# A two-layer graph block on one core: the barrier of 8 turned tiles a batch added by VectorE instead of TensorE

## The reference, cut to what matters

```python
h = relu(layernorm(x))
x = x + L0(h, adj)        # attention over the graph's edges, 8 heads of 16
h = relu(layernorm(x))
x = x + L1(h, adj)        # two similarity graphs on the same edges

# L0
q, k, v = split(h @ W_qkv + b_qkv)
scores = where(adj, q @ k.T / sqrt(16), -inf)     # per head, 512 x 512
y = softmax(scores) @ v ;  out = y @ W_out + b_out

# L1
z_l, z_g, v = h @ Wl, h @ Wg, h @ Wv
A_l = max(cos(z_l, z_l), 0)  without diagonal, only on edges
A_g = exp(-|z_g - z_g'|^2 / 2)  without diagonal, only on edges
K = 0.9 * A_l / rowsum(A_l) + 0.1 * A_g / rowsum(A_g)
out = K @ v @ Wo
```

## Time and profile before

| | |
|---|---|
| median of 3 runs | 866.05 us |
| the profiled execution | 870.53 us |
| its span, first to last instruction | 868.8 us |
| mean granted TensorE clock | 0.986 |
| TensorE matmuls busy | 799.0 us (92%), 4732 |
| weight loads busy | 450.8 us (52%) |
| VectorE busy | 684.9 us (79%), 1950 |
| ScalarE busy | 544.1 us (63%), 1230 |
| GpSimd busy | 707.4 us (81%), 829 |
| moved by DMA | 54.7 MB, 63 GB/s in the mean |

### The profile page before, as it was taken

One profiled execution on the slowest core, in us unless ns is written; L12 is line 12 of the kernel. 1 busy time (PEld: TensorE's weight loads), 2 busy tenths in 40 slices (PEclk: granted clock), 3 DMA queues, 4 the chain that ended last, 5 costly groups with the idle time before them and its releaser, 6 DMA issues.

```text
span 868.8 us, 15316 instructions
## 1 busy us (share of the span) xinstructions
PE 799.0 (92%) x4732; PEld 450.8 (52%) x4732; DVE 684.9 (79%) x1950; ACT 544.1 (63%) x1230; POOL 707.4 (81%) x829
## 2 busy tenths in 40 slices
PE   3769799999999999999999999999999999999886
PEld 2222245646464555656465564646455565645466
DVE  4666669888897979788796978879797988779266
ACT  4536495765758486674848566575857667575832
POOL 3268999797989889898888979898898989877921
PEclk9888999999999999999999999999999999999999
DMA  3331313113131412312141221303131231210000
GB/s 89 105 103 38 104 38 95 48 50 101 27 94 38 116 38 72 82 48 80 27 116 38 81 74 50 99 21 102 38 115 39 61 93 41 67 36 14 13 1 25
DMA packets 49840, 54.74 MB, mean 63 GB/s; under 512 B 7264, under 2 KB 43616, under 8 KB 49760
## 3 DMA queue, kind: packets, MB, share of 16 engines
q1 hardware_dynamic: 49760, 53.76, 22.0%
HBM read 30.28 MB, written 23.07 MB: 61 GB/s over the span
## 4 chain that ended last, share of the span: by engine, by line
PE 35%; POOL 30%; DMA 12%; DVE 8%; issue 7%; ACT 5%; SPq 2%; POOLq 0%; DVEq 0%; ACTq 0%
POOL probs_t L547 17%; PE adj L722 6%; DMA qk_rows<-k_dram 6%; PE pv L708 6%; PE score L680 5%; PE turned L694 4%; DMA k_dram<-split 4%; PE adj L717 4%; POOL split L579 3%; PE work L740 3%; POOL x_resid L615 2%; DVE scrap L955 2%; POOL split L577 2%; PE work L717 2%; PE turned L693 1%
## 5 line engine op out<-in xcount | busy, mean ns | idle before, releaser
L547 POOL TENSOR_TENSOR probs_t<-probs_t,keep_t 128x512 int32<-128x512 int32 x384 | 493.2, 1314 | 15.6 <-ACT probs_t L1126 15.5
L1126 ACT ACTIVATE probs_t<-turned 128x512 f32<-128x512 f32 x512 | 298.5, 603 | 186.1 <-PE turned L694 183.1
L955 DVE CUSTOM_DVE_ANT_0 scrap<-score,mask_add 128x512 f32<-128x512 f32 x512 | 341.0, 682 | 61.0 <-PE score L680 58.3
L680 PE MATMUL score<-qk_rows 96*128 96x512 bf16 x512 | 199.3, 389 | 15.1 <-DMA qk_rows<-k_dram 13.0
L694 PE MATMUL turned<-qk_rows 99*128 99x512 bf16 x512 | 196.5, 384 | 14.6 <-ACT probs_t L1126 12.4
L708 PE MATMUL pv<-probs_t,v_cols 128*32 128x512 f32 x1024 | 139.0, 615 | 3.9 <-POOL probs_t L547 3.9
L680 PEld LDWEIGHTS score<-qk_rows 96*128 96x128 bf16 x512 | 49.8, 97 | 131.0 <-DVE neg_max L955 58.0
L694 PEld LDWEIGHTS turned<-qk_rows 99*128 99x128 bf16 x512 | 50.7, 99 | 47.3 <-ACT probs_t L1126 22.7
L988 DVE SCALAR_TENSOR_TENSOR adj_rbf<-rbf_exp,mask_t 128x512 f32<-128x512 f32 x64 | 74.4, 1164 | 1.0 <-ACT rbf_exp L1160 1.0
L722 PEld LDWEIGHTS adj<-v_cos,adj_cos 128*128 128x128 f32 x480 | 61.4, 190 | 12.1 <-issue 4.7
L722 PE MATMUL adj<-v_cos,adj_cos 128*128 128x129 f32 x480 | 64.6, 276 | 0.7 <-DVE out_sb L1011 0.7
(11 more groups left out here) (159 smaller groups left out, 1188.4 us busy)
## 6 DMA issues: line engine op xcount, KB each, us to landing
q_dram<-split SPq DMA_DIRECT2D x96, 128.0 KB
qk_rows<-q_dram SPq DMA_DIRECT2D x32, 384.0 KB, 3.9
k_dram<-split SPq DMA_DIRECT2D x48, 128.0 KB
qk_rows<-k_dram SPq DMA_DIRECT2D x32, 192.0 KB, 4.3
x_sb<-in_x_dram SPq DMA_DIRECT2D x16, 256.0 KB, 3.5
qk_rows<-k_dram SPq DMA_DIRECT2D x32, 128.0 KB, 4.2
out_dram<-out_sb SPq DMA_DIRECT2D x15, 256.0 KB, 2.5
qk_rows<-k_dram SPq DMA_DIRECT2D x32, 64.0 KB, 4.4
```

The costliest lines, as they stand in the source:

```text
L547: pool.tensor_tensor(tile, tile, keep_t[:, w // HG % T, :], ALU.mult).then_inc(probs_masked.sem, 1)
L680: pe.matmul(score_bank[u % 2][:, :], qk_rows[0:ROWS, b % 2, 0, h, t * P:(t + 1) * P], qk_rows[0:ROWS, b % 2, 1, h, :], start=True, stop=Tr ...
L955: dve.tensor_tensor_reduce(scrap[:, u % 2, :], score_bank[u % 2][:, :], mask_add[:, u % T, :], -1.0, 3.0e38, ALU.add, ALU.min, neg_max[:, ...
L1126: act.activation(probs_t[:, k % 4, w % HG, :], turned_bank[w % 2][:, :], ACT.Exp, scale=SCALE).then_inc(probs_ready.sem, 1)
```

## The change

For the tiles with `w % 4 == 3` the matmul of the barrier is gone (`MASK_BY_PE` is empty; `MASK_BY_DVE` has them). VectorE reads the turned tile from its bank, adds `bar_t` and writes the sum to a new SBUF tile `barred`, of which there is one; the exp reads that. TensorE's turned tile two later waits for this add instead of the exp. The add stands in VectorE's list in the tile's own slot, right behind the scan of the slot. The scan's unused output `scrap` becomes bf16. And many entries of `AT` move, most by one slot, some by more: `k_split` from -9 to -14, `x_biased` from -14 to -12, on SyncE `qk_store` from -28 to -35, `rows` from (-8, -5) to (-27, -12), `x_next` from -24 to -31, `max_load` from (1, 25) to (-4, 17), `store` from 99 to 106. `AT_BEFORE_LAST` and `AT_LAST` stay.

```diff
-MASK_BY_PE = (3,)
+MASK_BY_PE = ()
+MASK_BY_DVE = (3,)
@@ AT
-    "hT": (-26,), "q": (-24,), "k": (-22,), "v": (-12,), "max_turn": (18, 32),
+    "hT": (-26,), "q": (-24,), "k": (-22,), "v": (-13,), "max_turn": (18, 32),
-    "z": (69, 71, 72, 73), "zgT": (76,), "col": (78,), "zlT": (79,), "rbf": (78, 83, 85, 87),
-    "cos": (81, 83, 84, 89), "mix_cos": (92, 95, 96, 97), "mix_rbf": (94, 95, 96, 98),
-
-    "ln_scale": (-28,), "hT_copy": (-26,), "q_hi": (-24,), "k_hi": (-22,), "max_copy": (18, 32),
-    "pv_copy": (42, 56), "yT_copy": (61,), "ln2_scale": (64,), "h2T_hi": (66,), "z_copy": (70, 71, 72, 74),
-    "z_sums": (71, 72, 74, 75), "zgT_hi": (75,), "col_copy": (78,), "zlT_hi": (79,), "rbf_exp": (80, 83, 87, 89),
-
-    "ln_moments": (-35,), "hT_split": (-26,), "q_rest": (-24,), "k_rest": (-21,), "v_add": (-12,),
-    "max_split": (13, 30), "y_scale": (57, 59), "x1": (62,), "ln2_moments": (63,), "h2T_lo": (67,),
-    "zgT_lo": (76,), "zlT_lo": (79,), "rbf_read": (78, 83, 85, 88), "cos_read": (81, 83, 87, 90),
-    "rbf_mask": (83, 84, 88, 92), "out": (94, 96, 97, 101),
-
-    "ln_rstd": (-31,), "q_split": (-23,), "k_split": (-9,), "x_biased": (-14,), "ln2_rstd": (62,),
-    "z_norms": (76,),
-
-    "qk_store": (-28,), "rows": (-8, -5), "x_next": (-24,), "max_load": (1, 25), "store": (99,),
+    "z": (70, 71, 72, 73), "zgT": (76,), "col": (78,), "zlT": (79,), "rbf": (79, 82, 84, 87),
+    "cos": (82, 83, 85, 90), "mix_cos": (93, 96, 97, 98), "mix_rbf": (94, 96, 97, 99),
+
+    "ln_scale": (-29,), "hT_copy": (-27,), "q_hi": (-25,), "k_hi": (-22,), "max_copy": (18, 31),
+    "pv_copy": (42, 57), "yT_copy": (59,), "ln2_scale": (65,), "h2T_hi": (66,), "z_copy": (70, 71, 72, 74),
+    "z_sums": (70, 72, 74, 75), "zgT_hi": (75,), "col_copy": (78,), "zlT_hi": (79,), "rbf_exp": (80, 82, 87, 89),
+
+    "ln_moments": (-37,), "hT_split": (-26,), "q_rest": (-24,), "k_rest": (-21,), "v_add": (-12,),
+    "max_split": (14, 30), "y_scale": (57, 59), "x1": (62,), "ln2_moments": (63,), "h2T_lo": (67,),
+    "zgT_lo": (77,), "zlT_lo": (80,), "rbf_read": (78, 83, 85, 88), "cos_read": (81, 83, 87, 90),
+    "rbf_mask": (83, 84, 88, 92), "out": (94, 97, 98, 100),
+
+    "ln_rstd": (-31,), "q_split": (-24,), "k_split": (-14,), "x_biased": (-12,), "ln2_rstd": (62,),
+    "z_norms": (77,),
+
+    "qk_store": (-35,), "rows": (-27, -12), "x_next": (-31,), "max_load": (-4, 17), "store": (106,),
@@ tiles
+        scrap = sb("scrap", [P, 2, N], BF16)
+        barred = sb("barred", [P, N])
@@ turned_scores (TensorE)
-                reached(pe, probs_ready, b, w - 1)
+                if (w - 2) % SLOTS in by_dve:
+                    reached(pe, barred_ready, *((b, by_dve.index(w - 2) + 1) if w >= 2 else (b - 1, len(by_dve))))
+                else:
+                    reached(pe, probs_ready, b, w - 1)
@@ VectorE, behind the scan of the slot
+                if hit := tile_due(s, LAG):
+                    b, w = hit
+                    if w in by_dve:
+                        reached(dve, turned_filled, b, w + 1)
+                        if w >= HG:
+                            reached(dve, probs_ready, b, w - HG + 1)
+                        else:
+                            reached(dve, probs_ready, b - 1, w - HG + 1 + SLOTS)
+                        dve.tensor_tensor(barred[:, :], turned_bank[w % 2][:, :], bar_t[:, w // HG % T, :],
+                                          ALU.add).then_inc(barred_ready.sem, 1)
@@ exp (ScalarE)
+                    src = turned_bank[w % 2]
+                    if w in by_dve:
+                        reached(act, barred_ready, b, by_dve.index(w) + 1)
+                        src = barred
+                    act.activation(probs_t[:, k % 4, w % HG, :], src[:, :], ACT.Exp,
```

More of the change, by code:

```diff
@@ L107, in graph_blocks @@
     by_pe = [w for w in range(SLOTS) if w % HG in MASK_BY_PE]
-    by_pool = [w for w in range(SLOTS) if w % HG not in MASK_BY_PE]
+    by_dve = [w for w in range(SLOTS) if w % HG in MASK_BY_DVE]
+    by_pool = [w for w in range(SLOTS) if w not in by_pe and w not in by_dve]
     def slots_of(name, batch):
@@ L182, in graph_blocks @@
         v_cols = sb("v_cols", [P, 3, T, H, 32])
-        scrap = sb("scrap", [P, 2, N])
+        scrap = sb("scrap", [P, 2, N], BF16)
+        barred = sb("barred", [P, N])
         neg_max = sb("neg_max", [P, GROUPS, HALF])
@@ L295, in graph_blocks @@
         turned_filled = signal("turned_filled", SLOTS)
+        barred_ready = signal("barred_ready", len(by_dve))
         probs_ready = signal("probs_ready", SLOTS)
@@ L701, in attend @@
                 reached(pe, probs_masked, b, sum(w < ends for w in by_pool))
-                if by_pe:
-                    reached(pe, probs_ready, b, 1 + max(w for w in by_pe if w < ends))
+                reached(pe, probs_ready, b, 1 + max(w for w in by_pe + by_dve if w < ends))
                 if j == 0:
@@ L874, in _ @@
                         reached(pe, probs_ready, b)
+                        reached(pe, barred_ready, b)
                     split_product(z_bank(b, t)[:, 0:3 * D],
@@ L1125, in _ @@
                         reached(act, pv_filled, b, k - 3)
-                    act.activation(probs_t[:, k % 4, w % HG, :], turned_bank[w % 2][:, :], ACT.Exp,
+                    src = turned_bank[w % 2]
[3 more added lines that the diff above has]
+                    act.activation(probs_t[:, k % 4, w % HG, :], src[:, :], ACT.Exp,
                                    scale=SCALE).then_inc(probs_ready.sem, 1)
```

## The result

The changed kernel takes 903.31 us (median of 4 runs, 900.34 to 904.41), the kernel before 866.89 us in the runs beside it. The ratio is 1.0415, with a 95% interval of 1.0385 to 1.0445. It is slower by 36 us, where 6 were forecast. The direction was right; the size was not, and the time lies outside the range. The profiled execution is the fastest of the four, 900.34 us, against 876.7 expected for it.

What follows compares the result with a forecast made beforehand. It took a GpSimd-VectorE loop, just under the DRAM loop, to bind next: 50.4 against 49.74 us a period, 14 x 0.66 = +9.2, head -4, tail +1, so 876.7 profiled, less 4.5: 872 us, range 853 to 885.

Steps and rivals of the forecast that it cites:

- loop over DRAM: Per-batch cycle: GpSimd's splits, DMA out and back as rows, TensorE's first slots; 49.7 us, to drop to about 44.
- Y: Stretch from VectorE's scan 19 to the end of scan 31: 20.80 us before, 21.8 forecast with three adds.
- X: Stretch from rbf_bias to VectorE's scan of tile 19: 6.71 us before, 7.4 forecast with one add.
- P: Stretch from the end of scan 31 to rbf_bias, taken as GpSimd's work: 21.2 us, shortest 20.88 plus 0.3 for q's residue.
- over 2.4: Sign of being right: GpSimd's max_parts at slot 30 still waits for VectorE, longer, over 2.4 us a batch.
- I take 0.8 off: Saving on the last masked rbf block before scan 31, GpSimd having run out of masks: 1.75 us to about 0.7.
- head: Start of the run: late first row loads go, then GpSimd limits; -4 us (0 to -6).
- tail: End of the run, from 702.25: last eight adds cost little, their matmuls leave; +1 us (-2 to +3).
- VectorE becomes the limit all over: Rival: adds in slots 0 to 13 no longer hidden; 51.6 us a period, 889 us; chance 0.13.
- The freed loop wins: Rival: opening the DMA path outweighs the adds; 49.2 us a period, 855 us; chance 0.27.
- TensorE was the limit: Rival: the removed barrier matmuls count everywhere, 28 us off, 838 us; chance 0.03.

Runs made afterwards that it cites:

- old_slots_early_k: Kernel before, barrier still on TensorE, only the seven entries moved that bring the split of k forward by five slots: 866.3 us, ratio 0.9974.
- new_slots_pe: Changed kernel with all its slots, but TensorE adds the barrier again and VectorE adds none: 881.3 us, ratio 1.0141.
- adds_in_p: Changed kernel, but VectorE adds the barrier only in slots 0, 4, 8 and 12, TensorE in 16, 20, 24 and 28: 873.6 us, ratio 1.0043.
- new_slots_none: Changed kernel's slots with the barrier of the eight tiles left out altogether, neither matmul nor add: 871.3 us, ratio 1.0028.
- old_slots_dve: Changed kernel's code, eight adds on VectorE, with the old table AT of the kernel before: 936.9 us, ratio 1.0780.
- early_k_sums_dve: Kernel before with the early split of k, and VectorE instead of ScalarE makes the squares and sums of z_sums in every batch: 933.9 us, ratio 1.0748.
- mix_back: Changed kernel with only mix_cos, mix_rbf and out put back to the slots of before: 922.5 us, ratio 1.0613.
- x_back: Changed kernel with zgT_lo, zlT_lo, z_norms, the first rbf and the first cos put back to their earlier slots: 915.2 us, ratio 1.0528.
- early_k_adds_in_p: Kernel before with the early split of k, VectorE adding the barrier in slots 0, 4, 8 and 12, TensorE in the others: 898.0 us, ratio 1.0334.

## Why the prediction was right or wrong

**Right.** The loop over DRAM goes: no wait for rows is left in the steady periods. The adds cost 0.69 us each, 0.61 in a run; three in Y, one in X, four hidden beside P (measured +1.82, +0.62, -0.06 against no barrier, with the luck in Y that is told above). The last masked rbf block, 1.75 us before, took 0.68 (467.43), as GpSimd was idle there. GpSimd still waits at slot 30 for scan 31, though 1.7 us a period instead of the over 2.4 that I gave as the sign. The direction.

**Wrong: P, "21.2: the shortest 20.88, and 0.3".** The step that failed is that P is GpSimd's own work, and with it the use of the shortest stretch as its floor. P is TensorE's row of work from slot 0 to 14, with short handovers. The shortest P was not a floor that a freed kernel returns to: in that batch TensorE had started the batch's first score 1.6 us before the end of scan 31, and the stretch began with that lead. TensorE's timeline has that score:

```profile
204.38 0.39 PE L680 MATMUL score<-qk_rows 96*128 96x512 bf16 x1 [0.49 <-DMA qk_rows<-k_dram]
```

The trace of before shows more of this than I had read. From the first score of a batch to `rbf_bias` it is 21.84 to 21.86 us in nine batches, while their P went from 21.29 to 23.32: P is that row of TensorE, less the lead (or more the lateness) with which it starts. Two batches, the first score on TensorE and then `rbf_bias` on GpSimd, with P 22.49 in the first and 23.32 in the second:

```profile
304.38 0.39 PE L680 MATMUL score<-qk_rows 96*128 96x512 bf16 x1 [0.87 <-DMA qk_rows<-k_dram]
...
326.22 0.22 POOL L623 TENSOR_SCALAR rbf_bias<-square_sum 128x4 f32<-128x4 f32 x1
```

```profile
404.61 0.39 PE L680 MATMUL score<-qk_rows 96*128 96x512 bf16 x1 [1.68 <-DMA qk_rows<-k_dram]
...
426.47 0.23 POOL L623 TENSOR_SCALAR rbf_bias<-square_sum 128x4 f32<-128x4 f32 x1
```

The two batches that started with a lead of over 1 us (1.09 and 1.58) both took 20.88, so something else holds P at 20.88 there; what it is was not measured.

Without the DMA's lateness the old slots settle at 21.90 (old_slots_early_k), with no lead. In the changed kernel the row is 23.15 us and the lead 1.12, which makes 22.03. So the 1.1 us that I had counted as more work of TensorE came (21.86 to 23.15), and a lead that I had not foreseen gave most of it back; my 0.3 stood for neither. Giving the four barriers beside P to VectorE is worth 0.60 us there (22.63 in new_slots_pe, 22.03 in adds_in_p). P was 0.83 us short.

**Wrong: X, "6.71 + 0.61 for the add + 0.1".** The add was 0.62. The rest, 0.49 instead of 0.1, is in the slots: `col` waits for VectorE's `zgT_lo`, which stands a slot later, and then VectorE waits 1.3 us for the first rbf block (1.0 before, for `col_term`). Short by 0.41. Moving those entries back did not return it, so the cause within X is only seen in the waits, not shown.

**Wrong: Y, "I take 0.8 off".** The term that was mis-sized is what the masked rbf blocks give back. The last one did give back 1.07 us, but I had left the other three as they were. The four took 1.24, 1.16, 0.67 and 1.75 us in a steady batch before (384.28 to 396.85) and 0.68, 1.69, 1.28 and 0.68 after (451.31 to 467.43): -0.49 in sum instead of -0.8. The other 0.2 to 0.3 us are VectorE's idle time in Y, 0.42 instead of 0.21. Measured 22.38 for 21.8, short by 0.58.

**The sum.** Per period 0.83 + 0.41 + 0.58 = 1.82 us, and in the mean, with a dear first one of 53.62, 52.39 against 50.4: over the twelve periods between the ends of scan 31 at 104.06 and 732.74 that is 23.9 us. The head gave 1.3 us instead of 4 (+2.7). What follows 732.74, in which two more periods were forecast at +0.66 each and the tail at +1, came out 0.7 shorter than before instead (-3.0). Together 23.6, which is 900.34 - 876.7. The last 7.7 us of the miss are in no term of the kernel: I took the median to lie 4.5 us under the profiled execution, as before, and it lies 3.0 over it; 0.2 is rounding.

```profile
104.06 0.08 DVE L964 DVE_READ_ACCUMULATOR2_ANT neg_max<- 128x1 f32 x1
...
732.74 0.08 DVE L964 DVE_READ_ACCUMULATOR2_ANT neg_max<- 128x1 f32 x1
```

**The rivals.** "VectorE becomes the limit all over" (51.6 a period, 889 us) was nearest in size, at a chance of 0.13, but not in kind: beside P the adds are hidden in the new slots. In the old slots they are not (P 24.55), though VectorE is busy only 18.4 us there: what they cost are the waits behind them. "The freed loop wins" rested on the same wrong floor. "TensorE was the limit" was dismissed too soon for P: there the barrier's matmuls do count, 0.60 to 0.65 us for four. Its 838 us needed them to count everywhere, and with all eight gone the new slots gave 49.84 a period and 871.3 us (new_slots_none). The range ended at 885 because both ends of P, X and Y were taken from the kernel before, and the retimed slots were priced only where I had a row.

## What to carry to other kernels

An instruction moved to another engine costs its time only in the stretches where that engine is last, so split one period into stretches by the engine that is last in each, and count the adds by stretch: four of these eight were free and the other four cost 2.4 us a period. To find who is last, don't take the engine that waits to be released at a stretch's start, nor the shortest stretch as a floor; look at the busy times of all engines inside it, and, if a run is to be had, put a little more work on one of them, and less. Then compare the waits and the durations inside the stretch too, and not its length alone: beside Y a wait of 0.5 us was hidden by masks that happened to be cheaper. And look at what stands behind the new wait in the list of the engine that waits: an add of 0.6 us came to more than twice that, by subtraction, where VectorE waited for a copy that stood behind the exp that waited for the add.

## What was not expected of the hardware

Squares of 128x128 on VectorE with both inputs in SBUF took 0.29 us with GpSimd idle, and 0.63 and 1.00 us in the mean beside GpSimd's masks, against 0.68 for a 128x512 scan with an input in PSUM. The masked rbf blocks of one batch of the changed kernel took 0.68, 1.69, 1.28 and 0.68 us (451.31 to 467.43). GpSimd was idle beside the last. Beside the first it was not: both started at 451.31, and there GpSimd's part of the split took 1.71 us instead of 1.16, so it was the one that was held up.

```profile
451.31 0.68 DVE L1008 SCALAR_TENSOR_TENSOR adj_rbf<-rbf_exp,mask_t 128x512 f32<-128x512 f32 x1
...
451.31 1.71 POOL L584 TENSOR_TENSOR split<-resid,split 128x512 bf16<-128x512 f32 x1
```

The granted clock was 1.00 in the steady periods of the kernel before, of the changed one and of the others that are not named here. It fell in parts of old_slots_dve (0.93 in P), early_k_sums_dve (0.84 in X, behind a wait of TensorE of 3.66 us), mix_back and x_back (0.93 in Y, in three periods each) and early_k_adds_in_p (0.93 in P, in one). In P of old_slots_dve that cost 0.5 us a period, 24.55 against 24.04.
